# First group of mix heads: who subtracts which weights, and when VectorE takes its small steps

## The reference

```python
xn = _layernorm(x)
x = x + gnn(xn, edges) + mix(xn)
x = x + ffn(_layernorm(x))

# mix: 16 heads of 64
q, k, v = split(xn @ Wqkv)
dots = q @ k.T * 64 ** -0.5
spiky = sigmoid(relu(k @ W1 + b1) @ W2 + b2)        # one gate per head and row
weights = softmax(dots * softmax(spiky)[:, :, :, None])
out = (weights @ v) @ Wout + bout

# gnn: two linear layers each for q, k, v, scores plus an edge mask, softmax, @ v, @ wo
mask[src, dst] = softplus(edge_type_weights)[edge_type - 1]   # -inf elsewhere; a later edge wins
```

## Time and profile before

| | |
|---|---|
| median of 3 runs | 782.43 us (782.07 to 783.72) |
| the profiled execution's own time | 780.38 us |
| its span, first to last instruction | 778.6 us |
| PE busy | 749.6 us (96%) |
| DVE busy | 489.0 us (63%) |
| ACT busy | 382.5 us (49%) |
| POOL busy | 172.1 us (22%) |
| memory traffic | 101 GB/s over the span |

### The profile page before, as it was taken

The page is one execution under the profiler, slowest core; times in us unless marked ns, Lnnn a source line. Parts: engine busy times, 40 slices in busy tenths (PEclk is TensorE's granted clock), DMA queues, the critical chain, the costliest instruction groups (busy, mean ns, idle before and its releaser), DMA issues.

```text
span 778.6 us, 12119 instructions
## 1 busy us (share of the span) xinstructions
PE 749.6 (96%) x4738; PEld 720.0 (92%) x4738; DVE 489.0 (63%) x935; ACT 382.5 (49%) x658; POOL 172.1 (22%) x139
## 2 busy tenths in 40 slices
PE   4998999999999999999999999997999999999998
PEld 3988999999999999999999999887999999999997
DVE  6878756774884777567676776656544554451542
ACT  5444655665564556576767554134343334431430
POOL 4724322312322220260312665200000000000000
PEclk9999999999999999999999999999999999999999
DMA  5511223123313331212131613321433233231302
GB/s 198 193 55 59 105 109 109 58 107 109 104 59 109 108 120 74 109 54 109 55 109 54 244 55 129 109 109 55 140 124 115 109 128 143 108 109 55 109 2 81
DMA packets 14389, 79.59 MB, mean 102 GB/s; under 512 B 3216, under 2 KB 3504, under 8 KB 5616
## 3 DMA queue, kind: packets, MB, share of 16 engines
q1 hardware_dynamic: 11088, 74.45, 26.3%
q0 software_dynamic: 2960, 4.26, 1.7%
q10 hardware_dynamic: 288, 0.14, 0.1%
HBM read 76.66 MB, written 2.19 MB: 101 GB/s over the span
## 4 chain that ended last, share of the span: by engine, by line
PE 81%; DVE 10%; ACT 6%; issue 2%; DMA 0%; DVEq 0%; ACTq 0%
PE g_bank L1412 45%; PE g_bank L1439 14%; PE o_bank L1495 4%; PE t_bank L1484 3%; DVE w_lo L862 2%; PE s_bank L1782 2%; PE s_bank L1472 2%; PE s_bank L1473 2%; ACT w_hi L493 2%; PE s_bank L1366 2%; PE g_bank L1366 2%; ACT q_st L530 1%; PE t_bank L1782 1%; ACT q_st L528 1%; DVE act_lo L950 1%
## 5 line engine op out<-in xcount | busy, mean ns | idle before, releaser
L1412 PE MATMUL g_bank<-act_hi,w_hi 128*128 128x384 f32 x632 | 220.1, 348 | 0.8 <-DVE k_st L904 0.8
L1412 PE MATMUL g_bank<-act_hi,w_lo 128*128 128x384 f32 x632 | 211.9, 335 | 0.0
L1412 PE MATMUL g_bank<-act_lo,w_hi 128*128 128x384 f32 x632 | 211.5, 335 | 0.0
L862 DVE TENSOR_TENSOR w_lo<-raw,w_hi 128x2048 fp32r<-128x2048 f32 x59 | 138.5, 2348 | 34.1 <-ACT w_hi L493 33.4
L493 ACT ACTIVATE w_hi<-raw 128x2048 fp32r<-128x2048 f32 x67 | 127.9, 1909 | 25.0 <-PE s_bank L1782 12.5
L1412 PEld LDWEIGHTS g_bank<-act_hi,w_hi 128*128 128x128 f32 x632 | 119.1, 188 | 3.8 <-issue 3.7
L1412 PEld LDWEIGHTS g_bank<-act_lo,w_hi 128*128 128x128 f32 x632 | 119.0, 188 | 0.0
L1412 PEld LDWEIGHTS g_bank<-act_hi,w_lo 128*128 128x128 f32 x632 | 118.6, 188 | 0.0
L416 POOL DMA_INDIRECT edge_table<-ew,eidx x51 | 63.4, 1244 | 151.1 <-DMA edge_table<-ew,eidx 148.3
L1004 DVE TENSOR_TENSOR pT_lo<-t_bank,pT_hi 128x384 fp32r<-128x384 f32 x96 | 50.5, 552 | 26.1 <-ACT pT_hi L594 25.5
L365 POOL TENSOR_TENSOR w_lo<-raw,w_hi 128x2048 fp32r<-128x2048 f32 x9 | 42.3, 4700 | 101.3 <-ACT w_hi L493 101.3
(11 more groups left out here) (258 smaller groups left out, 1546.5 us busy)
## 6 DMA issues: line engine op xcount, KB each, us to landing
raw<-wstream_dram SPq DMA_DIRECT2D x68, 1024.0 KB, 4.8
x_sb<-x_dram SPq DMA_DIRECT2D x3, 512.0 KB, 4.7
y_acc<-x_dram POOLq DMA_DIRECT2D x3, 512.0 KB, 5.7
out_dram<-out_sb SPq DMA_DIRECT2D x6, 256.0 KB, 2.0
edge_table<-ew,eidx POOLq DMA_INDIRECT x51, 2.2
edge_table<-mask POOLq DMA_DIRECT2D x1, 576.0 KB, 3.5
mask<-edge_table POOLq DMA_DIRECT2D x1, 576.0 KB, 4.2
bo_b<-bo_dram POOLq DMA_DIRECT2D x1, 512.0 KB, 7.2
```

The costliest lines, as they stand in the source:

```text
L862: V.tensor_tensor(flat(w_lo[s][:, :, :]), raw[:, s, :], flat(w_hi[s][:, :, :]), ALU.subtract) \
L1412: last = mm(out, w2[a], x2[b], start=k == 0 and a + b == 0, stop=not after and k == KT - 1 and a == 1)
```

## The change

Nothing is computed otherwise; instructions change places, and one subtraction changes engine.

1. Unit 4 joins `ON_POOL`: POOL subtracts it, directly behind unit 3, and DVE no longer does. SP's wait ahead of unit 6 is on POOL's count now.
2. POOL waits for `row_v` 2 (the gate rows of group 0 are scaled) before it subtracts unit 3.
3. In unit 0, ACT takes the first half of the key between its exp and its ln, and DVE takes its part behind key tile 0, ahead of the edge weights; the ln's partner steps move behind.
4. Key tiles move: PE has four of them in unit 2 (at m, k = 0,0; 0,4; 1,0; 1,5) where there were three, and three in unit 3 where there were four. On DVE tile 6 stands ahead of `row_third`, tile 8 ahead of `take_alpha` and tile 9 ahead of the second query half.
5. The first head's scores are issued inside the V unit, behind its second tile's k = 6, and no longer behind the tile. ACT takes the first exp ahead of V's first half. DVE takes the maxima ahead of V's first half, and scales two score tiles ahead of V's second half.
6. In unit 4 PE transposes the first head's tiles 0 and 1 behind k = 1 (was 2), issues the next scores behind k = 2 (was 4, behind the transposes), and transposes tile 2 behind k = 3 (was 4). ACT evicts all three transposed tiles ahead of the next exp.
7. At the ends of groups 0, 1, 2, ACT's `exp_row` and DVE's `row_third` stand ahead of the first query half.

```diff
-ON_POOL = (U_A0, mix_v(0), U_GNN + 4, U_GNN + 5, U_GNN + 7, U_GNN + 8, U_GNN + 10, U_GNN + 11, U_OUT + 1)
+ON_POOL = (U_A0, mix_v(0), mix_v(0) + 1, U_GNN + 4, U_GNN + 5, U_GNN + 7, U_GNN + 8, U_GNN + 10, U_GNN + 11, U_OUT + 1)
...
                 own.done(nc.gpsimd.tensor_tensor(ew[:, :], ew[:, :], code, ALU.add))
+            pool.wait_ge(row_v, 2)
             split_lo(mix_v(0))
+            split_lo(mix_v(0) + 1)
             pool.wait_ge(key_free, KEY_TILES)
...
             nc.scalar.activation(wtmp, wtmp, ACT.Exp, scale=-1.0).then_inc(soft_a, 1)
+            take_K(Index(U_K0), 0, None)
             act.wait_ge(soft_v, 2)
             nc.scalar.activation(wtmp, wtmp, ACT.Ln).then_inc(soft_a, 1)
-            for m in range(2):
-                take_K(Index(U_K0), m, None)
+            take_K(Index(U_K0), 1, None)
             act.wait_ge(half_ready, 1)
...
-                take_pT(tile, (0, 1))
-                if h < HG - 1:
+                if (g.base, h) == (0, 0):
+                    take_pT(tile)
                     exps("mix", g, h + 1, (0,))
-                take_pT(tile, (2,))
+                else:
+                    take_pT(tile, (0, 1))
+                    if h < HG - 1:
+                        exps("mix", g, h + 1, (0,))
+                    take_pT(tile, (2,))
                 split_hi(n + 1)
...
                 else:
+                    exps("mix", g, 0, (0,))
                     take_V(n, 0)
-                    exps("mix", g, 0)
+                    exps("mix", g, 0, (1, 2))
                 take_V(n, 1)
...
                     tanh_row(g + 1)
+                    exp_row(g + 1)
                     take_Q(n + 5, 0, None)
-                    exp_row(g + 1)
                     take_alpha(g + 1)
...
             key_tile(0)
+            take_K(Index(U_K0), 0, None)
+            key_tile(1)
             dve.wait_ge(soft_a, 1)
             V.tensor_scalar(wtmp, wtmp, 1.0, None, ALU.add).then_inc(soft_v, 1)
-            key_tile(1)
+            dve.wait_ge(w1_ready, 1)
+            V.tensor_tensor(w1_lo[:, :], w1_raw[:, :], w1_hi[:, :], ALU.subtract).then_inc(w1_ready, 1)
             dve.wait_ge(soft_a, 2)
             own.done(V.tensor_scalar(wtmp2, etw, 0.0, None, ALU.max))
             own.done(V.tensor_tensor(wtmp2, wtmp2, wtmp, ALU.add))
             V.tensor_scalar(w8, wtmp2, 1.0 / ATT_SCALE, None, ALU.mult).then_inc(soft_v, 1)
-            dve.wait_ge(w1_ready, 1)
-            V.tensor_tensor(w1_lo[:, :], w1_raw[:, :], w1_hi[:, :], ALU.subtract).then_inc(w1_ready, 1)
-            take_K(Index(U_K0), 0, None)
+            take_K(Index(U_K0), 1, None)
             key_tile(2)
-            take_K(Index(U_K0), 1, None)
             split_lo(Index(U_Q0))
...
             take_chain(0, 1)
+            key_tile(6)
             row_third(Index(0))
-            key_tile(6)
             key_tile(7)
             take_Q(Index(U_Q0), 0, None)
+            key_tile(8)
             take_alpha(Index(0))
-            key_tile(8)
+            key_tile(9)
             take_Q(Index(U_Q0), 1, None)
-            for c in range(9, KEY_TILES):
+            for c in range(10, KEY_TILES):
                 key_tile(c)
...
                 if gi == 0:
-                    split_lo(n + 1)
+                    maxima("mix", g, 0)
                     take_V(n, 0)
-                    maxima("mix", g, 0)
+                    normals("mix", g, 0, (0, 1))
                     take_V(n, 1)
-                    normals("mix", g, 0)
+                    normals("mix", g, 0, (2,))
                 else:
...
                     split_lo(n + 6)
+                    row_third(g + 1)
                     take_Q(n + 5, 0, None)
-                    row_third(g + 1)
                     take_alpha(g + 1)
...
             def in_Q(m, k):
-                if (m, k) in ((0, 2), (0, 7), (1, 4)):
-                    key_tiles(6 + ((0, 2), (0, 7), (1, 4)).index((m, k)))
+                if (m, k) in ((0, 0), (0, 4), (1, 0), (1, 5)):
+                    key_tiles(6 + ((0, 0), (0, 4), (1, 0), (1, 5)).index((m, k)))
                 if (m, k) == (1, 2):
                     weights_T(first)
             def in_V(t, k):
-                if (t, k) in ((0, 1), (0, 5), (1, 1), (1, 5)):
-                    key_tiles(9 + ((0, 1), (0, 5), (1, 1), (1, 5)).index((t, k)))
+                if (t, k) in ((0, 1), (0, 5), (1, 1)):
+                    key_tiles(10 + ((0, 1), (0, 5), (1, 1)).index((t, k)))
+                if (t, k) == (1, 6):
+                    pe.wait_ge(key_free, KEY_TILES)
+                    head_scores("mix", first, 0)
...
                     gemm_N(n, act_hi, act_lo, T_X, 0, between=in_V)
-                    pe.wait_ge(key_free, KEY_TILES)
-                    head_scores("mix", g, 0)
                 gemm_N(n, act_hi, act_lo, T_X, 1)
...
                         if (gi, h) == (0, 0):
+                            if k == 1:
+                                head_T("mix", g, h, tile, (0, 1))
                             if k == 2:
-                                head_T("mix", g, h, tile, (0, 1))
-                            if k == 4:
+                                head_scores("mix", g, h + 1)
+                            if k == 3:
                                 head_T("mix", g, h, tile, (2,))
-                                head_scores("mix", g, h + 1)
                         else:
```

## The result

The changed kernel takes **776.52 us** (median of 5 runs, 776.45 to 776.89); the kernel before, beside it on the same chip, 782.07 (5 runs, 780.17 to 783.72). The ratio is 0.9931, its 95% interval 0.9917 to 0.9944: faster by 0.7%. The forecast was 777.2, its range 775.5 to 780.0. The profiled execution took 776.48 us, with a span of 774.7.

The account below looks back on a forecast made before the run. PE, busy 96% of the span, bounds the kernel, so only gaps between its matmuls can give: 5.56 us in reach, less a remaining 0.35, is 5.2; 782.43 - 5.2 = 777.2 us, range 775.5 to 780.0.

Parts of the forecast that it names:

- Gate rows: PE's gap at the gate transposes, waiting for DVE's scaled rows (L1031): it goes, gaining 0.84 us.
- First scores: PE's gap at the first scores, waiting for key tiles: 0.83 us, of which a wait of 0.35 us stays.
- First transposes and `head_out`: PE's gaps at the first score transposes and the first head_out: both go, gaining 1.49 and 0.54 us.
- L974 held: First softmax's small DVE product, taken as held to the end of POOL's unit 4 subtraction: 0.6 us, costing nothing.
- Group ends: PE's waits for gate rows at three group ends: 3 x 0.30 = 0.90 us gained.
- First key half: PE's gap at the second unit's start, waiting for DVE's first key half (L904): it goes, gaining 0.96 us.
- A: Rival: the hold moves with POOL to L974, for longer; one to two us go again, 778.7 us; chance 0.15.
- B: Rival: the first head stays late, gaps at first transposes and head_out reappear; 779.2 us; chance 0.10.
- C: Rival: what PE gains by 73 us it waits for in the next heads or elsewhere; 782.4 us; chance 0.07.
- D: Rival: POOL holds DVE whatever DVE does, key tiles included; 4.1 us lost again, 781.3 us; chance 0.02.
- E: Rival: slower, POOL's indirect DMAs make the edge table late if turns exceed 4.8 us; up to 836; chance 0.03.
- if PE's total up to 80 us moves by less than 4 us: Stated sign of being wrong: PE's total up to 80 us moves by less than 4 us.

Follow-up runs that it names:

- e6: Kernel before plus one line: POOL waits for the scaled gate rows before subtracting unit 3; 781.62 us, ratio to before 0.9993.
- e7: Changed kernel with key tile 10 moved from unit 3 into unit 2 on PE and ahead of DVE's second query half; 777.23 us, ratio 0.9944.
- e8: From e7: ACT rounds unit 4's weights ahead of the second query half, DVE takes all key tiles ahead of that half; 775.86 us, ratio 0.9923.
- e1: Changed kernel with unit 4's w_lo subtraction back on DVE, ahead of the first maxima; 778.05 us, ratio to the kernel before 0.9954.
- e5: Changed kernel with the first scores behind V's second tile again and the old places in unit 4; 777.76 us, ratio 0.9946.
- e3: Changed kernel with the old order at the ends of groups 0, 1 and 2 (query half ahead of gate rows); 778.26 us, ratio 0.9959.
- e4: Changed kernel with the old order of the key halves in unit 0 on ACT and DVE; 776.70 us, ratio 0.9938.
- e0_full: The changed kernel run once more, unaltered, as control beside the later runs; 776.95 us, ratio to the kernel before 0.9938.
- b0_before: The kernel before, unaltered, traced a second time to look at its start; 781.91 us (1 run).
- e2: Changed kernel without POOL's wait for the gate rows before subtracting unit 3; 777.52 us, ratio to the kernel before 0.9954.

## Why the prediction was right, and which term was mis-sized

Times of the trace after are compared with those expected less 1.65 us, by which PE's first L1412 matmul (22.10 before, 23.75 after) came later.

- *Gate rows, 0.84.* Right. L1038 takes 0.41 us in all four executions, and e6 measures the one line at 0.80. Undone alone in the changed kernel it costs 0.38 from B to F, since more of PE's work now lies ahead of the transposes.
- *First scores, 0.83 less a remaining wait of 0.35.* Right. The gap is 0.50 from start to start where it was 1.00; the wait left is 0.33 against the pitch of 0.17. It stands at 59.59, which is 57.94 without the later start, for 58.1 expected. The pitch itself was wrong here: where PE does not wait, e7 and e8 have 0.12 from V's matmul to the scores, so that both gaps are 0.05 larger and their difference is the same.
- *First transposes and `head_out`, 1.49 + 0.54.* Right in sum. B to F gained 3.47; less 0.80 and 0.50 that leaves 2.17 for these two, where 2.03 were forecast. Which of the moves closes the larger gap is open (e1 and e5). PE's transposes of the next head stand at 75.40, 73.75 without the later start, for 73.7.
- *L974 held.* Right in kind, nearly in size: 0.55 us where 0.6 were taken, once in three. The row could not be read from the trace of before. It cost nothing in this version, as the prediction said; e7 shows it as the bound 0.35 us further on, and e8 takes it away.
- *Group ends, 0.90.* Right: 0.98 from F to I, and 0.91 in e3.
- *First key half, 0.96.* **This term was mis-sized.** The text read "The gap goes: 0.96", from a trace in which PE started earlier than in any other. The gap is the difference of two times that move apart by chance: PE's arrival (27.17 there) and the end of DVE's chain behind POOL's subtraction. In the second trace of the same kernel PE arrives at 28.50 and there is no gap; in e4 the old order costs 0.25, in e6 0.08. (Of the 1.19 us from S to B in the first trace, 0.96 is the gap and 0.08 the slower matmul behind it; 0.15 lies in PE's eight matmuls from S on, ahead of it, where nothing was changed.) The mechanism was right, since the old order did hold the eviction, but in three of the four traces that have this order PE comes hardly before it, or after it.
- *Rivals.* A did not happen, but was the next in line by 0.35 us (e7). B did not: no wait at either place. C did not: the gained time was kept through 489 us. D did not: eight of the last eleven comparisons began beside POOL's third subtraction and took 0.34 or 0.35 us each, like the others, and the key tiles ended at 59.5. E did not: the 51 indirect DMAs ran from 63.4 to 293.8, (293.8 - 63.4) / 50 = 4.6 us each where it was 4.2, under the 4.8 that I had set as the limit. The turns vary by themselves: in e0_full the last began at 284.3, and in b0_before, the old kernel, at 283.4 and not 275.2. The gnn's first maximum came at 314.92 without a wait for the mask, which had landed at 302.85.

One sign of being wrong that the prediction named was met as it stands: "if PE's total up to 80 us moves by less than 4 us". The next head's transposes came 2.87 us earlier (78.27 and 75.40). Counted from S they moved by 4.66 us against the first trace of the kernel before, but by 3.48 against its second: what is missing there is the key term. The span tells the same. It was forecast at 773.4 us and is 774.7. From S to I the first comparison gives 5.64 us, but the changed trace reached S 1.80 us later, which leaves 3.84.

With the key term at 0.03 to 0.25 the parts make 4.5 to 4.7 us; the medians say 5.55 (first comparison) and 5.35 (e0_full against 17 runs). The difference lies within the interval of the ratio, 4.4 to 6.5 us. A likely cause is the clock that an execution got in one short stretch (last section): among the executions whose mean granted clock was 1.000, twelve of the kernel before have spans of 778.6 to 779.5 us (median 779.1) and three of the changed one 774.4, 774.7 and 774.7, so that like beside like they are 4.4 apart. (Such a span still holds the chance of the start: one of e1, a slower kernel by its marks, is 774.2.) So the sum of 5.2 was some 0.6 too high for what the change does in most executions, and the forecast came out within 0.7 us of the median partly by luck: a gain read from one execution with an early start was taken off the median of others.

L1031 and L1074 (SBUF to SBUF) and L981 (two SBUF inputs, 128x1) are held to POOL's end, in e7 to within 0.02 us, while maxima, comparisons and `q_lo`'s subtraction, whose first input is a PSUM bank, keep their time beside POOL (the maximum at 60.25 took 0.56, `q_lo` in e8 1.12). The Trainium skill, SBUF — State Buffer, "SBUF: two separate sides", says that a GpSimd instruction and a DVE one in a 2-port mode or with two SBUF inputs exclude each other on a port pair, for the length of the one that started first. L981's rows agree with it; whether L1031 and L1074 run in such a mode, no trace shows.

The prediction's words for the held steps, "from SBUF to SBUF", are too wide. In the trace of before this reciprocal, on DVE, began while POOL's subtraction ran (43.64 to 48.23), and took what it takes alone:

```profile
44.12 0.15 DVE L1030 RECIPROCAL small<-small 4x1 f32<-4x1 f32 x1 [1.77 <-ACT row_e L621]
```

It reads and writes SBUF and is not held; b0_before and e2 show the same. What sets it apart was not tested.

## What to carry to other kernels

If a gap is the difference between two chains that start from different things (here PE from a transfer and its own pace, DVE from POOL's end), one trace gives one sample of it: look at a second trace of the same kernel before costing it. Measure experiments from a mark behind the start to a mark ahead of the next uncertain stretch; here that turned a scatter of some 2 us into one of 0.1 or less. And if a small step on DVE is held by a long one on POOL, move POOL's start, not the small step: a one-line wait gave 0.8 us, and rounding the weights earlier on ACT, together with the key tiles' new places, gave the last 0.45.

## What was not expected of the hardware

Near 530 us, where PE stands still once for 2.15 us and once for 1.4 to 1.6, the granted clock of PE falls in some executions from 1.00 (2.4 GHz) to 0.50 (1.2 GHz) and in some not. The windows of PE: stretch, us, busy (instructions), granted clock, DMA share, GB/s. First the changed kernel, then e0_full, which is the same program, then e1_fifth_on_dve:

```profile
528.00:530.00 2.00, 2.00 (x31) 1.00 0.00 0
530.00:532.00 2.00, 0.43 (x6) 1.00 0.45 94
532.00:534.00 2.00, 2.00 (x28) 1.00 1.01 426
```

```profile
528.00:530.00 2.00, 2.00 (x16) 0.50 0.00 0
530.00:532.00 2.00, 0.73 (x4) 0.72 0.93 291
532.00:534.00 2.00, 1.85 (x26) 1.00 0.55 234
```

```profile
530.00:532.00 2.00, 2.00 (x13) 0.54 0.19 33
532.00:534.00 2.00, 0.59 (x7) 0.50 0.81 303
534.00:536.00 2.00, 2.00 (x21) 0.50 0.45 188
```

From I to the last matmul's start the three take 281.60, 282.84 and 283.91 us: no fall, a short one (1.2 us lost) and a longer one (2.3 us lost). The wait of 2.15 us stands in all three, so it does not decide by itself. The kernel before shows the same (281.63 in the first trace, 282.78 in b0_before). This is a large part of the scatter between executions, and nothing in the change touches it.

The start shows a similar thing without the clock's column saying so: PE's first eight matmuls of 128x384 took 2.20 us in the first trace, 2.48 in e0_full and 2.90 in the changed kernel's, 0.32 us each from start to start at the slow pace where 0.17 is the pace later, with the granted clock at 1.00 in all. S goes with it: 20.57, 21.45 and 22.37 in these three, so the length of the slow pace is most of what I called chance. What decides when that pace ends was not tried.
